# Dense features loaded later and turned inside the third pass; eight gathers held back in two groups of four

## What is computed

```
e = stack([tbl_f[ids[:, f]] for f in range(26)], axis=1)         # 512 x 26 x 128
c = concatenate([dense[:, None], e], axis=1)                     # 512 x 27 x 128
z = concatenate([dense, einsum('bnd,bmd->bnm', c, c)[:, i < j], dense], axis=1)   # 512 x 607
h = maximum(z @ W_top1 + b_top1, 0)                              # 512 x 512
h = maximum(h @ W_top2 + b_top2, 0)                              # 512 x 256
y = h @ W_top3                                                   # 512 x 1
```

## Time and profile before

| | us |
|---|---|
| median of 3 runs | 134.91 |
| lowest and highest | 133.58, 135.23 |
| the profiled execution | 134.64 |
| its span in the trace | 132.1 |
| PE busy in the span | 110.6 (84%) |
| DVE, ACT, POOL busy | 83.8, 77.6, 59.6 |
| mean granted TensorE clock | 0.974 |

### The profile page before, as it was taken

The page is one execution under the profiler, slowest core; times in us unless marked ns, Lnnn a source line. Parts: engine busy times, 40 slices in busy tenths (PEclk is TensorE's granted clock), DMA queues, the critical chain, the costliest instruction groups (busy, mean ns, idle before and its releaser), DMA issues.

```text
span 132.1 us, 2612 instructions
## 1 busy us (share of the span) xinstructions
PE 110.6 (84%) x1036; PEld 94.5 (72%) x1036; DVE 83.8 (63%) x161; ACT 77.6 (59%) x146; POOL 59.6 (45%) x57
## 2 busy tenths in 40 slices
PE   0032996999999999999999189949989997999992
PEld 0022654868888888888888099849978996899891
DVE  5422399999999998897932507954950683095101
ACT  3019972499795959598584307945960776067120
POOL 2087878879788979878778400004700000000000
PEclk9999999999999999999999855999999999999999
DMA  4999976939888785881211100000110000000000
GB/s 96 275 406 390 347 264 186 297 118 212 342 207 330 202 336 191 261 314 56 56 48 46 53 0 5 0 5 7 52 25 0 5 0 0 5 0 5 0 0 1
DMA packets 6492, 16.99 MB, mean 129 GB/s; under 512 B 1617, under 2 KB 2897, under 8 KB 6354
## 3 DMA queue, kind: packets, MB, share of 16 engines
q1 hardware_dynamic: 4274, 13.38, 29.5%
q0 software_dynamic: 1536, 3.15, 8.7%
q10 hardware_dynamic: 672, 0.32, 1.0%
HBM read 16.83 MB, written 0.00 MB: 127 GB/s over the span
## 4 chain that ended last, share of the span: by engine, by line
POOL 41%; PE 25%; issue 17%; DVE 9%; DMA 5%; ACT 2%
POOL rows L306 41%; PE dots_ps L620 8%; DVE z L324 8%; PE acc_ps L647 8%; DMA ids_sb<-ids 4%; PE turn_ps L661 3%; PE acc_ps L638 2%; PE turn_ps L593 2%; ACT z L348 1%; PE acc_ps L661 1%; PE turn_ps L671 1%; DVE cols L316 1%; PE acc_ps L671 1%; DMA rows<-tbl,ids_sb 1%; ACT h L427 0%
## 5 line engine op out<-in xcount | busy, mean ns | idle before, releaser
L306 POOL DMA_INDIRECT rows<-tbl,ids_sb x48 | 58.7, 1222 | 35.0 <-PE turn_ps L593 16.4
L465 DVE TENSOR_SCALAR onehot<-ids_row,row_number 128x1024 fp32r<-128x1024 int32 x49 | 33.2, 745 | 4.3 <-PE acc_ps L568 3.1
L324 DVE COPY z<-dots_ps 30x128 f32<-30x128 f32 (+5 forms) x80 | 21.0, 263 | 8.8 <-issue 5.6
L348 ACT ACTIVATE z<-dots_ps 30x128 f32<-30x128 f32 (+5 forms) x80 | 19.7, 246 | 11.5 <-PE dots_ps L620 10.3
L620 PE MATMUL dots_ps<-cols 128*64 128x52 f32 x512 | 18.9, 240 | 6.3 <-DMA rows<-tbl,ids_sb 3.2
L620 PEld LDWEIGHTS dots_ps<-cols 128*64 128x64 f32 x512 | 18.2, 156 | 7.5 <-issue 5.6
L560 PE MATMUL acc_ps<-onehot,table_hi 128*128 128x512 f32 x68 | 18.7, 422 | 3.1 <-ACT table_hi L348 3.1
L475 DVE TENSOR_TENSOR table_lo<-table_raw,table_hi 128x2048 fp32r<-128x2048 f32 (+1 forms) x8 | 16.6, 2079 | 4.8 <-ACT table_hi L348 4.8
L560 PEld LDWEIGHTS acc_ps<-onehot,table_hi 128*128 128x128 f32 x68 | 13.0, 200 | 8.3 <-ACT table_hi L348 4.2
L568 PE MATMUL acc_ps<-onehot,table_lo 128*128 128x512 f32 x68 | 17.4, 408 | 1.0 <-DVE table_lo L475 1.0
L348 ACT ACTIVATE cols<-turn_ps 128x512 f32<-128x512 f32 x10 | 10.6, 1082 | 10.4 <-PE turn_ps L593 10.4
(11 more groups left out here) (42 smaller groups left out, 72.0 us busy)
## 6 DMA issues: line engine op xcount, KB each, us to landing
table_raw<-picked_tables SPq DMA_DIRECT2D x14, 512.0 KB, 7.0
ids_row<-ids_picked SPq DMA_DIRECT2D x7, 512.0 KB, 5.1
table_raw<-w SPq DMA_DIRECT2D x1, 1536.0 KB, 8.4
rows<-tbl,ids_sb POOLq DMA_INDIRECT x48, 3.7
w_sb<-w SPq DMA_DIRECT2D x1, 512.0 KB, 12.5
dense_sb<-dense ACTq DMA_DIRECT2D x1, 256.0 KB, 6.8
table_raw<-picked_tables SPq DMA_DIRECT2D x2, 128.0 KB, 5.8
ids_sb<-ids ACTq DMA_DIRECT2D x1, 52.0 KB, 5.3
```

Source lines behind the costliest of these rows:

```text
L306: nc.gpsimd.indirect_dma_start(rows[:, t % GATHER_RING, n, :], None, tables[f][:, :], index).then_inc(rows_in[t][g], 16)
L324: last = copy(z[QUAD * q:QUAD * q + rows_of, t % 2, :, QUAD * s + b0:QUAD * s + b1], src.rearrange("i b c -> i c b"))
L348: return nc.scalar.activation(dst, src, ACT.Copy)
L465: nc.vector.tensor_scalar(onehot[:, c], ids_row[:, pair % IDS_RING], row_number[first_row][:, c:c + 1], None, ALU.is_equal).then_inc(oneho ...
```

## The change

Five things are changed. The values computed are the same.

1. The dense features' load moves from ACT's queue, where it was second, to SP's, behind the tables of pass 2. Its rows are put in order on the host, as are those of w2, and the two small weights become one transfer.
2. PE turns the dense features in pass 2, between its high and its low matmuls, not ahead of the first pass. ACT's three copies of them move one each into iterations 3, 4 and 5 of its loop. The first use of the PSUM bank by a gathered group waits for all three.
3. ACT's order at the start is written out: round the tables of pass 0, then make pass 1's one-hot chunk, then round pass 1's tables.
4. POOL stops twice: group (3, 1) waits for the dot products of tiles 0 and 1, group (3, 2) for those of tile 2. `dots(0)` now waits for (2, 2) and (3, 0) to have landed, `dots(2)` for (3, 1).
5. In iteration t = 1, PE turns (3, 2) after layer 2, and ACT moves it after `activate2`.

The diff, cut where only a count or a name follows:

```diff
@@ -64,10 +64,11 @@
 GATHER_RING = 3
 PICK_TURNS = {NP - 3: [(0, 0)], NP - 2: [(0, 1)], NP - 1: [(0, 2), (1, 0)]}
-
-
-PAUSES = {(3, 2): 1}
-LANDED_FIRST = [(3, 0), (3, 1)]
+DENSE_PASS = 2
+
+
+PAUSES = {(3, 1): 1, (3, 2): 2}
+LANDED = {0: [(2, 2), (3, 0)], 2: [(3, 1)]}
...
@@ -256,13 +257,14 @@
                     src = picked_tables[r0:r0 + P * n].rearrange("(p c) d -> p c d", c=n)
                     sp.dma_start(table_raw[:, slot, 0:n], src).then_inc(table_in[slot], 16)
-            for p in range(PASS_RING):
-                if PASSES[p][3] and PASSES[p][0] < IDS_RING:
-                    load_ids_row(PASSES[p][0])
-                load_tables(p)
-            sp.dma_start(w2_sb[:], w2.rearrange("(k p) o -> p k o", p=P)).then_inc(w2_in, 16)
-            sp.dma_start(w3_sb[:], w3).then_inc(small_in, 16)
-            sp.dma_start(b2_sb[:], b2).then_inc(small_in, 16)
+            load_ids_row(0)
+            load_tables(0)
+            load_tables(1)
+            load_ids_row(1)
+            load_tables(2)
+            sp.dma_start(dense_sb[:], dense).then_inc(dense_in, 16)
+            sp.dma_start(w2_sb[:], w2).then_inc(w2_in, 16)
+            sp.dma_start(last_sb[:], last_weights).then_inc(small_in, 16)
             for pair in range(IDS_RING, PAIRS):
                 p = FIRST_PASS[pair]
                 if p >= PASS_RING:
@@ -342,7 +344,6 @@
         @block.scalar
         def _(act):
             act.dma_start(ids_sb[:], ids).then_inc(ids_in, 16)
-            act.dma_start(dense_sb[:], dense.rearrange("(t p) d -> p t d", p=P)).then_inc(dense_in, 16)
             def copy(dst, src):
                 return nc.scalar.activation(dst, src, ACT.Copy)
@@ -387,25 +388,34 @@
             def move_group(t, g):
                 move_turned("scalar", act.wait_ge, copy, t, g)
-            act.wait_ge(dense_turned, 1)
-            dense_turned_ps = turn_ps[0][:].rearrange("d t b -> d (t b)")
-            copy(dense_t[:].rearrange("d (h e j) -> d h e j", e=2, j=QUAD),
-                 dense_turned_ps.rearrange("d (h j e) -> d h e j", e=2, j=QUAD))
-            copy(cols[:, :, 0], dense_turned_ps)
-            copy(cols[:, :, NODES + REPEATS.index(0)], dense_turned_ps).then_inc(dense_moved, 1)
+            def move_dense(part):
+
+                turned_ps = turn_ps[0][:].rearrange("d t b -> d (t b)")
+                if part == 0:
+                    act.wait_ge(dense_turned, 1)
+                    copy(dense_t[:].rearrange("d (h e j) -> d h e j", e=2, j=QUAD),
+                         turned_ps.rearrange("d (h j e) -> d h e j", e=2, j=QUAD)).then_inc(dense_moved, 1)
+                else:
+                    slot = 0 if part == 1 else NODES + REPEATS.index(0)
+                    copy(cols[:, :, slot], turned_ps).then_inc(dense_moved, 1)
+
             split_hi(0)
-            for p in range(NP):
-                if ACT_CHUNKS[p]:
+            measure(1)
+            finish_onehot(1)
+            split_hi(1)
+            for p in range(1, NP):
+                if p >= 2:
                     measure(p)
                 if p + 1 < NP:
                     split_hi(p + 1)
-                if ACT_CHUNKS[p]:
+                if p >= 2:
                     finish_onehot(p)
-                if p >= 1:
-                    for t, g in PICK_TURNS.get(p - 1, ()):
-                        move_group(t, g)
-                    if PASSES[p - 1][4]:
-                        move_picked(PASSES[p - 1][0])
+                for t, g in PICK_TURNS.get(p - 1, ()):
+                    move_group(t, g)
+                if PASSES[p - 1][4]:
+                    move_picked(PASSES[p - 1][0])
+                if p - DENSE_PASS in (1, 2, 3):
+                    move_dense(p - DENSE_PASS - 1)
             for t, g in PICK_TURNS.get(NP - 1, ()):
                 move_group(t, g)
             act.wait_ge(last_done, 1)
...
@@ -442,11 +452,15 @@
                 if t + 1 < TILES:
                     evacuate(t + 1, 0, 0)
                 activate1(t)
-                for g in range(2, NG):
-                    move_group(t + 2, g)
+                if t == 0:
+                    for g in range(2, NG):
+                        move_group(t + 2, g)
                 if t + 1 < TILES:
                     evacuate(t + 1, 0, 2)
                 activate2(t)
+                if t >= 1:
+                    for g in range(2, NG):
+                        move_group(t + 2, g)
         @block.vector
         def _(dve):
...
@@ -560,6 +572,8 @@
                         last = nc.tensor.matmul(sums[i], table_hi[:, p % 2, i, c, :], onehot[:, c, i, :],
                                                 start=first and c == 0, stop=False)
                 last.then_inc(hi_used, 1)
+                if p == DENSE_PASS:
+                    turn_dense()
                 for t, g in PICK_TURNS.get(p, ()):
                     turn(t, g)
                 pe.wait_ge(lo_ready, p + 1)
@@ -578,13 +592,19 @@
                             last = low(i, c)
                         last.then_inc(last_done, 1)
+            def turn_dense():
+                pe.wait_ge(dense_in, 16)
+                for t in range(TILES):
+                    last = nc.tensor.transpose(turn_ps[0][:, t, :], dense_sb[:, t, :], identity[:])
+                last.then_inc(dense_turned, 1)
+
             def turn(t, g):
                 if t >= TILES:
                     return
                 m = t * NG + g
                 pe.wait_ge(rows_in[t][g], 16 * len(GROUPS[g]))
                 if m == 1:
-                    pe.wait_ge(dense_moved, 1)
+                    pe.wait_ge(dense_moved, 3)
                 if m >= 2:
                     before = ((m - 2) // NG, (m - 2) % NG)
                     engine = mover(*before)
@@ -597,12 +617,12 @@
             def dots(t, between=None):
                 if t == 0:
-                    pe.wait_ge(dense_moved, 1)
+                    pe.wait_ge(dense_moved, 3)
                     pe.wait_ge(picked_moved, NUM_PICKED - 2)
                     pe.wait_ge(first_moved, 2)
                     pe.wait_ge(cleared, 2)
-                    for u, g in LANDED_FIRST:
-                        pe.wait_ge(rows_in[u][g], 16 * len(GROUPS[g]))
+                for u, g in LANDED.get(t, ()):
+                    pe.wait_ge(rows_in[u][g], 16 * len(GROUPS[g]))
                 if t == 1:
                     pe.wait_ge(rest_moved, 2)
                 for engine in ("scalar", "vector"):
...
@@ -673,10 +693,6 @@
                 last.then_inc(layer3_done, 1)
             pe.wait_ge(identity_ready, 1)
-            pe.wait_ge(dense_in, 16)
-            for t in range(TILES):
-                last = nc.tensor.transpose(turn_ps[0][:, t, :], dense_sb[:, t, :], identity[:])
-            last.then_inc(dense_turned, 1)
             for p in range(NP):
                 pick(p)
             for g in range(NG):
@@ -701,10 +717,10 @@
                 if t + 1 == TILES:
                     layer3(t - 1)
                 layer1(t, range(H1_ACT))
+                layer1(t, (H1_ACT,))
+                layer2(t)
                 for g in range(2, NG):
                     turn(t + 2, g)
-                layer1(t, (H1_ACT,))
-                layer2(t)
             layer3(TILES - 1)
@@ -739,15 +755,15 @@
             padded[r0:r0 + len(part)] = part
     out = nc.dram_tensor("out_y", (BATCH, 1), F32, kind="ExternalOutput").ap()
     build(nc,
-          declare("dense", np.asarray(inputs["r_dense_features"])[order]),
+          declare("dense", np.asarray(inputs["r_dense_features"])[order].reshape(TILES, P, DIM).transpose(1, 0, 2)),
           declare("ids", ids.reshape(TILES, P, NUM_TABLES).transpose(1, 0, 2)),
           declare("ids_picked", ids[:, PICKED].T.reshape(PAIRS, 2, BATCH)),
           declare("picked_tables", padded),
           {f: declare(f"tbl_{f}", inputs[f"tbl_{f}"]) for f in GATHERED},
           declare("w1", w1),
-          declare("w2", inputs["W_top2"]),
-          declare("w3", np.asarray(inputs["W_top3"]).reshape(K2, P).T),
-          declare("b2", np.asarray(inputs["b_top2"]).reshape(K2, P).T),
+          declare("w2", np.asarray(inputs["W_top2"]).reshape(K1, P, H2).transpose(1, 0, 2)),
+          declare("last_weights", np.stack([np.asarray(inputs["W_top3"]).reshape(K2, P).T,
+                                            np.asarray(inputs["b_top2"]).reshape(K2, P).T], axis=1)),
           out)
     result = run_bass_kernel_spmd(nc, [arrays], core_ids=[0])
     return result.results[0]["out_y"]
```

More of the change, by code:

```diff
@@ L144, in pieces_before, with build @@
     return sum(len(pieces_of(u)) for u in range(t))
-def build(nc, dense, ids, ids_picked, picked_tables, tables, w1, w2, w3, b2, out):
+def build(nc, dense, ids, ids_picked, picked_tables, tables, w1, w2, last_weights, out):
     with ExitStack() as ctx:
@@ L161, in build @@
         w2_sb = sb("w2_sb", [P, K1, H2])
-        w3_sb = sb("w3_sb", [P, K2])
-        b2_sb = sb("b2_sb", [P, K2])
+        last_sb = sb("last_sb", [P, 2, K2])
```

(7 more changed lines are left out.)

## The result

The changed kernel ran in 129.8 us (median of 4, 128.71 to 130.49) against 135.07 before (median of 4): ratio 0.964, 95% interval 0.952 to 0.975. Forecast was 128.7 with 126.8 to 131.7. On two other occasions the same comparison gave 0.949 (0.943 to 0.955) and 0.972 (0.966 to 0.978), apart by more than their intervals. The ratios are of fast runs alone; the traces of "old order at t = 1" and of "stops one place earlier" are of slow executions, so nothing that only they show is taken as shown.

The account below looks back on a forecast made before the run. POOL's gather issue was taken to bound the front half, with PE waiting for the last landing before dots(0). Gains 5.35 + 1.58 - 0.75 = 6.2 from 134.64 gave 128.45, with 0.27 to the median 128.7; range 126.8 to 131.7.

Parts of the forecast that it names:

- POOL bounds the front, and the landing of (3, 0) is the last wait: Ahead of dots(0): gather issue sets the pace; (3, 0) lands at 70.58, after PE is free at 70.3, at best 69.6.
- the first stop's own worth: Before dots(0): four gathers leave the stretch, so dots(0) can start at 70.94, 5.35 earlier.
- POOL's pace: Gathers in the passes: no change taken, with 1.0 either way for how they meet DVE's subtractions.
- PE's start: Pass 0: PE's first high matmul near 8.8 to 8.9 instead of 12.27, 3.4 earlier; perhaps 0.7 better, not counted.
- Earlier than 69.6 PE cannot be, so the gain is at most 1.3 more: Before dots(0): PE's earliest finish of the passes caps any extra gain from faster POOL at 1.3.
- ACT's copies at zero cost: Three passes: each dense copy, 0.94 to 1.06, fits ACT's idle 1.38; cost zero, without that cover up to 1 each.
- Clock: dots(0): PE's shorter idle keeps full clock; 2.08 + 0.09 to the first move instead of 3.75, 1.58 gained.
- Rival B: Halves of dots: the clock falls all the same, 1.67 for each slow half waited for; 130.4 to 132.0; chance 0.14.
- if the clock fell: Sign of being wrong: the forecast expected granted clock 1.00 throughout from dots(0) on.
- Gathers behind dots(1) hidden by 0.75: Before dots(2): (3, 1) lands 7.0 after dots(1) ends, dots(2) starts 7.77 after, so no cost.
- 0.75 given back at t = 1: Before dots(3): turning and ACT's move of (3, 2) after layer 2 put dots(3) at 111.75 against 110.99.
- rival E: At the two stops: slower, if gathers between DVE's moves took 2.94, not 0.94; 143; chance 0.04.

Follow-up runs that it names:

- old order at t = 1: Changed kernel with both stops, but PE and ACT handle (3, 2) where they did before the change; ratio 0.962 (0.952 to 0.972).
- stops one place earlier: Changed kernel with (3, 1) after dots(0), (3, 2) after dots(1), old order at t = 1, no landing wait before dots(2); 132.46 us, ratio 0.972.
- the two halves of the change alone: Kernel before plus stops, landing waits and new t = 1 order: 134.32 us, 0.999; changed kernel with those three as before: 132.17 us, 0.982.
- no late gathers: Changed kernel without gathers (3, 1) and (3, 2) and the waits for their landing, tile 3 computed from leftover buffers; 126.39 us, ratio 0.930.
- the second one of the changed kernel: Changed kernel run again with no edit, the second of two repeats; 131.95 us, ratio 0.972 to the kernel before.
- the first trace of before: Kernel before, no edit: the profiled execution on which the forecast was made; 134.64 us.

## Why the prediction was right, and where its terms were not

**POOL bounds the front, and the landing of (3, 0) is the last wait: right**, shown by the releaser of dots(0) and by the two halves of the change alone. Held against the row, the first stop's own worth was 5.31 where 5.35 was forecast: 7.62 earlier in all, 2.31 of it because POOL's fortieth gather came earlier.

**POOL's pace: "I take no change", off by 2.31.** 1.59 of it is the ids' landing (first gather at 4.77, not 6.36), which the working did not price although the dense load stood beside it in the change; the packets of 512 B were the larger part. The other 0.72 is within the 1.0 allowed, and is of the kind named there: seven gathers of each trace take 1.9 or more, 16.4 together before and 15.5 after, with none of 2.94 among them. It depends on where the gathers fall: in three more traces with this start ("no late gathers", "old order", "stops one place earlier") the first gather stood at 4.89 to 5.36, another gather took 2.56 and not 1.90, the fortieth came at 66.92 to 67.43, and PE waited 1.8 to 1.9 ahead of dots(0).

**PE's start: 3.4 earlier forecast, 5.5 measured** (6.75 against 12.27). I had named 0.7 for the dense load and taken nothing. It is not worth anything by itself: PE still waits 0.69. But it undoes a bound of the working, "Earlier than 69.6 PE cannot be, so the gain is at most 1.3 more": PE was free at 67.98, and the gain in front was 2.3 more.

**ACT's copies at zero cost: right.** The one-hot chunk in passes 3 to 5 is never what PE waits for. **Clock: right in this trace**, 2.17 for 3.75. The gap of 1.78 before the second half of dots(1) lowered it in no trace. Ahead of dots(2) it did fall in other executions, the second one of the changed kernel among them: PE had stood idle 1.0 to 1.1, made ten matmuls in 1.38 and stood idle 1.76, and in six of seven traces with this pattern the first half of dots(2) then took 3.3 to 3.7. Rival B's fall exists, at another place, by way of the late hand-overs, and "if the clock fell" was one of the prediction's own signs of being wrong.

**Gathers behind dots(1) hidden by 0.75: wrong.** Not because the rows land late (no trace of the changed kernel names a landing before dots(2)), but because what PE feeds reaches ACT and DVE late while gathers run. Cost 0.4 to 2.3, and 1.5 more where the clock follows. **0.75 given back at t = 1: the size was wrong**, 2.05. The handovers account for 0.46 (d23 9.12 without gathers), the gathers for 1.6. My rival E looked for slower gathers; they kept to 0.94. The harm ran the other way, from POOL to the others, and no rival had that.

**The time came out partly by luck.** The forecast saw 6.2 of gain, the profiled executions differ by 5.9: 2.3 more in front, 2.8 less behind, 0.4 less at the output's transfer, 0.6 more outside the span. The error in front alone would have given 126.4, those behind alone 131.9, both outside the range of 126.8 to 131.7.

No kernel timed beside the changed one was faster. Of the four timed on the chip without it, the fastest leaves gathers out and computes wrong values; the ratios of the others lie within the changed kernel's three (0.949 to 0.972) or above.

## What to carry to other kernels

Moving background gathers off a wait is not free because their issue fits in a gap: look at who hands over to whom while they run. Here the runs of gathers in the layers delayed what ACT and DVE take over from TensorE, mostly until 1.0 to 1.2 us after the last of them, so the place to put them is where nothing waits for TensorE. Two runs of four did better than one of eight (old order in both, same chip: 0.962, 0.952 to 0.972, against 0.982, 0.973 to 0.992). A wait removed on one engine pays only if the next in line has moved too: 1.8% and 0.1% apart, 5.1% together. And one trace is one execution: look at the second before you call a slack of 0.75 us cover.

## What the hardware showed that I had not expected

- While POOL issued indirect gathers in the fp32 part, ACT and DVE took over from PE up to 2.1 us late (7 us with eight gathers), mostly until 1.0 to 1.2 us after the last gather's end (1.7 with eight; in the first trace of before nothing was late); without gathers they did at once. In the passes, where gathers run as densely, ACT's one-hot chunk followed PE's last low matmul within 0.2 of PE's next set (41.38 and 41.18 in the earlier trace rows). Whether signals or matmuls are held, which part of a gather holds them, and why the passes are spared, was not settled: one kernel's trace shows matmuls stopping, the others show them on time and only their readers late.
- 256 KB in 512 B pieces, issued on ACT's queue 0.4 us behind a 52 KB load, delayed that load by 1.0 us more than the same 256 KB in 2 KB pieces (first gather at 5.90, not 4.92; one trace each).
